# A Perceiver layer on one core: the attention product in one PSUM bank, three banks for projections, another order of steps

## The reference

```python
x = x + cross_attention(layernorm(x), ctx, ctx, mask)   # 16 heads of 16 features, 1601 keys
x = x + span_attention(layernorm(x))                    # 64 positions, scores from a learned distance
x = x + ffn(layernorm(x))                               # shared gated MLP and two hashed experts

# cross attention, all matmuls in float32 accuracy
qh, kh, vh = heads(q @ wq.T + bq), heads(ctx @ wk.T + bk), heads(ctx @ wv.T + bv)
scores = einsum('bhqd,bhkd->bhqk', qh, kh) / 4          # masked with -1e9
out = einsum('bhqk,bhkd->bhqd', softmax(scores), vh)
return merge_heads(out) @ wo.T + bo
```

## Time and profile before

| | us |
|---|---|
| median of 3 runs | 1679.22 |
| lowest and highest run | 1673.58, 1679.73 |
| the profiled execution | 1684.18 |
| its span, first to last instruction | 1682.3 |
| TensorE busy | 1557.7 (93%) |
| VectorE busy | 1049.9 (62%) |
| ScalarE busy | 924.1 (55%) |
| GpSimd busy | 425.0 (25%) |

### The profile page before, as it was taken

The page is one execution under the profiler, slowest core; times in us unless marked ns, Lnnn a source line. Parts: engine busy times, 40 slices in busy tenths (PEclk is TensorE's granted clock), DMA queues, the critical chain, the costliest instruction groups (busy, mean ns, idle before and its releaser), DMA issues. The chain is left out here.

```text
span 1682.3 us, 56731 instructions
## 1 busy us (share of the span) xinstructions
PE 1557.7 (93%) x23644; PEld 1275.9 (76%) x23644; DVE 1049.9 (62%) x3925; ACT 924.1 (55%) x1832; POOL 425.0 (25%) x549
## 2 busy tenths in 40 slices
PE   7699999999999999999999999999999757886997
PEld 2578888888888888888888888888888613333997
DVE  5666666666666666666666666666666446552543
ACT  4355555565555555555565556555555514554553
POOL 0132332222222333323233222222232030000520
PEclk9899999999999999999999999999999978887999
DMA  5433344444444443334334444444443050000111
GB/s 145 138 102 103 104 106 122 124 111 113 110 112 117 110 117 105 105 104 105 104 104 104 120 126 111 112 112 113 112 111 80 9 149 1 1 1 1 51 33 51
DMA packets 101904, 157.94 MB, mean 94 GB/s; under 512 B 56943, under 2 KB 65903, under 8 KB 101376
## 3 DMA queue, kind: packets, MB, share of 16 engines
q1 hardware_dynamic: 101456, 153.69, 34.4%
q0 software_dynamic: 192, 0.59, 0.1%
HBM read 69.17 MB, written 4.19 MB: 44 GB/s over the span
## 5 line engine op out<-in xcount | busy, mean ns | idle before, releaser
L674 DVE CUSTOM_DVE_ANT_0 junk<-bank,mask_q 128x400 bf16<-128x400 f32 (+1 forms) x1024 | 559.0, 571 | 138.9 <-issue 132.3
L626 ACT ACTIVATE probs<-bank 128x512 f32<-128x512 f32 (+1 forms) x832 | 451.1, 595 | 237.9 <-PE bank L786 212.1
L602 POOL CAST ctx_hi<-ctx_raw 128x400 fp32r<-128x400 f32 x248 | 121.6, 519 | 898.2 <-PE bank L750 898.2
L665 DVE SCALAR_TENSOR_TENSOR k_lo<-bank,bk,k_hi 128x400 f16<-128x400 f32 (+1 forms) x256 | 162.4, 634 | 247.3 <-ACT k_hi L636 247.3
L767 PE MATMUL bank<-kstack,qstack 96*128 96x400 f16 (+1 forms) x1024 | 296.8, 339 | 11.4 <-DVE part_max L674 3.8
L750 PE MATMUL bank<-wv_hi,ctx_hi 128*128 128x256 f32 (+1 forms) x832 | 284.3, 342 | 14.4 <-DVE k_lo L665 14.4
L786 PE MATMUL bank<-qstack,kstack 104*128 104x128 f16 (+1 forms) x3328 | 257.9, 220 | 4.1 <-ACT probs L626 3.4
L605 POOL TENSOR_TENSOR ctx_lo<-ctx_raw,ctx_hi 128x400 fp32r<-128x400 f32 x248 | 253.3, 1042 | 0.0
L786 PEld LDWEIGHTS bank<-qstack,kstack 104*128 104x128 f16 (+1 forms) x3328 | 209.1, 99 | 51.0 <-issue 21.6
L646 ACT ACTIVATE v<-bank 128x256 f32<-128x256 f32 (+1 forms) x416 | 159.7, 384 | 148.4 <-PE bank L750 148.3
L636 ACT ACTIVATE k_hi<-bank,bk 128x400 f16<-128x400 f32 (+1 forms) x256 | 152.4, 595 | 158.6 <-PE bank L740 154.2
(11 more groups left out here) (165 smaller groups left out, 1767.0 us busy)
## 6 DMA issues: line engine op xcount, KB each, us to landing
ctx_raw<-in_ctxT SPq DMA_DIRECT2D x32, 1602.0 KB, 7.0
kstack<-k_hi SPq DMA_DIRECT2D x512, 100.1 KB, 2.2
kstack<-k_lo SPq DMA_DIRECT2D x256, 100.1 KB, 2.2
weight<-in_w SPq DMA_DIRECT2D x18, 256.0 KB, 2.7
x<-in_xT SPq DMA_DIRECT2D x8, 512.0 KB, 6.1
attn_out<-o_norm SPq DMA_DIRECT2D x256, 8.0 KB, 1.8
qstack<-q_parts SPq DMA_DIRECT2D x192, 16.0 KB
out_yT<-x SPq DMA_DIRECT2D x1, 2048.0 KB, 6.4
```

What stands on the lines that cost most here:

```text
L602: nc.gpsimd.tensor_copy(c_hi[:, k, s0:s0 + n], raw[:, k, s0:s0 + n]).then_inc(ctx_hi, 1)
L626: nc.scalar.activation(probs[kt % NP][0:m, GROUPS * h:GROUPS * (h + 1), :], st[h][0:m, :], ACT.Exp, scale=DK ** -0.5 / (UP * UP)).then_inc ...
L665: nc.vector.scalar_tensor_tensor(k_lo[:, t, s0:s0 + n], pj[(b.slot + c) % 2][:, 0:n], w["bk"][:, t:t + 1], k_hi[:, t, s0:s0 + n], ALU.add, ...
L674: nc.vector.tensor_tensor_reduce(junk[(b.slot + i) % 2][:, 0:n], sm[(b.slot + i) % 2][:, 0:n], w["mask_q"][:, s0:s0 + n], 1.0, -3.0e38, AL ...
```

## The change

- `ob` is one bank in place of two. A new step O has VectorE copy the finished product of the batch before out of it, to `o_raw` in SBUF (`copy_out`); the first product of a batch waits for that copy (`o_copied`).
- The bank that this frees goes to `pj`: three banks, `bank[0]`, `bank[1]` and `bank[4]`. `sm` becomes `bank[5:7]`. A projection now waits for the one three before it.
- `outputs` works in SBUF on half the columns. The two heads of a pair are joined with two columns of zeros and ones (`half_rows`, a new constant), then the sums are shuffled and inverted, and the last product writes `attn_out` directly. `store` and its 8 DMAs a turn are gone, and the output projection in `tail` waits for `out_done`.
- `SLOTS` is new, so all engines have another order.

```diff
-    pj = bank[0:2]
+    pj = bank[0:2] + bank[4:5]
     st = bank[2:4]
-    sm = bank[4:6]
-    ob = bank[6:8]
+    sm = bank[5:7]
+    ob = bank[7]
...
-    SLOTS = ["K S0 S1 L K", "K S0 S1 K", "K S0 S1 K P P", "K S0 S1 K V",
-             "M V M S0 S1 M V M M P P", "M M S0 S1 M V M", "H M V M S0 S1 M V M M P P", "M M S0 S1 M V M",
-             "H M V M S0 S1 M V M M P P", "M M S0 S1 M V M", "H M V M S0 S1 M V M M P P", "S0 S1 G T V N",
-             "H S0 S1 P P"]
+    SLOTS = ["K K K S0 L S1", "K S0 S1", "K K S0 S1 O K K", "S0 M P P P M M S1", "V S0 M S1 M P M V", "M M V M S0 H M S1 V",
+             "M S0 M V M M P P S1 M M", "V M S0 V M S1 V M V M H", "M S0 S1 M V M", "M S0 V M M S1 V", "S0 M P P M M H V M S1",
+             "V S0 M M S1 P P P G H", "P T S0 N S1"]
...
-            if cur and cur.n >= 2:
-                store(at(cur.n - 2))
...
+        def copy_out(b):
+
+            dve.wait_ge(pv_done, KT * (b.n + 1))
+            nc.vector.tensor_copy(o_raw[:], ob[:, 0:GROUPS * S].rearrange("p (k e c) -> p k e c", k=NK, e=2)).then_inc(o_copied, 1)
+
         def outputs(b):
-            o = ob[b.slot][:, 0:GROUPS * S].rearrange("p (t c) -> p t c", t=GROUPS)
-            dve.wait_ge(pv_done, KT * (b.n + 1))
-            for e in range(2):
-                nc.vector.stream_shuffle(sums[:, e::2, :], o[:, e::2, :], [DK * (1 - e) + i % DK for i in range(32)]).then_inc(sums_done, 1)
-            dve.wait_ge(sums_done, 2 * (b.n + 1))
-            nc.vector.reciprocal(rsum[:], sums[:]).then_inc(rsum_done, 1)
+
+
+            o = [o_raw[:, :, e, :] for e in range(2)]
+            low, high = w["half_rows"][:, 0:1], w["half_rows"][:, 1:2]
+            dve.wait_ge(o_copied, b.n + 1)
+            nc.vector.tensor_scalar(o_half[:], o[1], high, None, ALU.mult).then_inc(halves_done, 1)
+            nc.vector.tensor_scalar(sum_half[:], o[0], high, None, ALU.mult).then_inc(halves_done, 1)
+            dve.wait_ge(halves_done, 2 * (b.n + 1))
+            nc.vector.scalar_tensor_tensor(o_both[:], o[0], low, o_half[:], ALU.mult, ALU.add).then_inc(both_done, 1)
+            nc.vector.scalar_tensor_tensor(sum_both[:], o[1], low, sum_half[:], ALU.mult, ALU.add).then_inc(both_done, 1)
+            dve.wait_ge(both_done, 2 * (b.n + 1))
+            nc.vector.stream_shuffle(sum_half[:], sum_both[:], [(i + DK) % 32 for i in range(32)]).then_inc(sums_done, 1)
+            dve.wait_ge(sums_done, b.n + 1)
+            nc.vector.reciprocal(rsum[:], sum_half[:]).then_inc(rsum_done, 1)
             dve.wait_ge(rsum_done, b.n + 1)
-
-            need(dve, attn_st[b.slot], 16 * STORE_DMAS * (b.used - 1))
-            nc.vector.tensor_tensor(o_norm[b.slot][:], o, rsum[:], ALU.mult).then_inc(out_done, 1)
+            nc.vector.tensor_tensor(attn_out[:, :, b.n * S:(b.n + 1) * S], o_both[:], rsum[:], ALU.mult).then_inc(out_done, 1)
...
-            if j < 2:
-                need(pe, v_done, KT * (b.n - 1) + KT - 1 + j)
-            elif j - 2 < NCK:
-                pe.wait_ge(klo_done, NCK * b.n + j - 1)
+            if j < PJ:
+                need(pe, v_done, KT * (b.n - 1) + KT - PJ + 1 + j)
+            elif j - PJ < NCK:
+                pe.wait_ge(klo_done, NCK * b.n + j - PJ + 1)
             else:
-                pe.wait_ge(v_done, KT * b.n + j - 1 - NCK)
+                pe.wait_ge(v_done, KT * b.n + j - PJ + 1 - NCK)
...
             if kt == 0:
 
-                need(pe, out_done, b.n - 1)
+                need(pe, o_copied, b.n)
...
         def output_a(c, _):
-            for stored in attn_st:
-                pe.wait_ge(stored, 16 * STORE_DMAS * (CB // 2) * (c + 1))
+            pe.wait_ge(out_done, CB * (c + 1))
```

More of the change, by code:

```diff
@@ L47 @@
 VB = 3 * DK
-STORE_DMAS = 2 * GROUPS
 EPS = 1e-5
@@ L120, in build @@
         bo_all = ctx.enter_context(nc.sbuf_tensor("bo_all", [P, NK], F32))
-        attn_st = [sem(f"attn_st{i}") for i in range(2)]
+        out_done = sem("out_done")
         eps_col = ctx.enter_context(nc.sbuf_tensor("eps_col", [P, 1], F32))
@@ L263, in sync @@
             load(bo[:], ins["bo"], wo_in)
+            load(w["half_rows"][:], ins["c_half_rows"], wo_in)
             for c in range(NCH):
@@ L566, in lay_out_keys @@
                                  part[32 * g:32 * g + 32, t, :]).then_inc(kstack_in[b.slot][p], 16)
-        def store(b):
-            sp.wait_ge(out_done, b.n + 1)
-            for g in range(GROUPS):
-                for e in range(2):
-                    rows = slice(32 * g + DK * e, 32 * g + DK * (e + 1))
-                    sp.dma_start(attn_out[rows, :, bass.ds(b.n * S, S)], o_norm[b.slot][rows, e::2, :]).then_inc(attn_st[b.slot], 16)
         sp.wait_ge(first_in["stack_zero"], 2)
@@ L590, in sync @@
         turns(sp, turn)
-        for n in (B - 2, B - 1):
-            store(at(n))
     def gpsimd(pool):
@@ L712, in turn @@
                         shift_in(nxt)
+                    if what == "O" and cur and not first(cur):
+                        copy_out(before(cur))
                     if what == "N" and cur and not first(cur):
@@ L772, in turn_shift @@
             pe.wait_ge(max_found, b.n + 1)
-            nc.tensor.matmul(sm[b.slot][0:PAIRS, 0:P], row_max[:], w["turn_down"][:], start=True, stop=True).then_inc(shift_rows, 1)
+            nc.tensor.matmul(sm[SHIFT_BANK][0:PAIRS, 0:P], row_max[:], w["turn_down"][:], start=True, stop=True).then_inc(shift_rows, 1)
         def scores(b, kt, h, masked):
@@ L800, in products @@
                     c0 = VB * p + DK * e
-                    mm = nc.tensor.matmul(ob[b.slot][32 * g:32 * g + 32, t * S:(t + 1) * S],
+                    mm = nc.tensor.matmul(ob[32 * g:32 * g + 32, t * S:(t + 1) * S],
                                           v[b.slot][0:m, kt, c0:c0 + 2 * DK], probs[kt % NP][0:m, p, S * e:S * (e + 1)],
@@ L936, in _, with span_attention @@
                 mlps["tensor"](pe)
[L939 removed]
+def span_attention(nc, own, bank, sem, mean_w, eps_col, attn_out, out_done, x, h2, wo, bo_all, wspan, wval, wout,
                    sel_a, sel_b, head_ones, x_in, w_in, sel_in, h2_done):
@@ L1511, in constants @@
     return {
+        "c_half_rows": (rows[:, None] % 32 // DK == np.arange(2)[None]).astype(np.float32),
         "c_ident": np.eye(P, dtype=np.float32),
```

54 lines of the change are left out of this document (31 added, 23 removed).

## The result

| | before | after |
|---|---|---|
| median | 1678.88 us | 1627.93 us |
| lowest and highest of 4 runs | 1673.58, 1679.73 | 1625.23, 1629.14 |
| ratio, 95% interval | | 0.9701, 0.9677 to 0.9725 |
| profiled execution, its span | 1684.18, 1682.3 | 1627.13, 1624.9 |

The change saves 51 us, where 42.9 were forecast (1637 us, range 1618 to 1660). I take the span apart by the same marks as in the prediction: the first and the last T, TensorE's last matmul of the last turn, the first matmul of the next part.

A forecast was written before the change was run, and what follows sets the result against it. TensorE, busy 93% of the span, sets the end, with short stalls and passages to win. Terms: 31 x (0.72 + 0.40 + 0) = 34.7, + 5.7 + 2.0 + 0.5 = 42.9 us saved; forecast 1637 us, range 1618 to 1660.

The forecast's parts named there:

- Third bank: Projection V1 waits for K7's low part with two projection banks; a third bank removes that stall, 0.72 us a turn.
- M's waits: M steps wait for VectorE's maximum, 0.75 us a turn; spreading them over the slots leaves 0.35, a gain of 0.40.
- Passages: Cost on TensorE of passing between kinds of step; the new order's changes sum to 0 a turn, bounds -0.3 and +0.5 us.
- One P run -0.1: Entry in the passage sum: the new order has one run of P steps less, saving 0.1 us a turn.
- N and K3: Normalizing on VectorE takes 2.6 us, with the copy 3.0, hidden while K3 finds K0's low part done; cover 0.4 us.
- rival (a): Waits come back elsewhere, before K3 and M0, with dearer V after S: gain 0.6 us a turn, 1652 us; chance 0.15.
- Slices and M0: M0 moves up to 12.0 us behind T; its key slice lands at 11.4, so cover is 0.6 us.
- Stores: Eight store DMAs a turn leave SP's queue: nothing gained within a turn, 5.7 us less in the gap to the next part.
- Last turn: From last T to TensorE's end, set by ScalarE's exponentials: 24.4 becomes 22.4 us, -2.0, bounds -3 and 0.
- First turn: Three projection banks save two short waits for `k_lo` in the first turn, -0.5 us.
- Rival (b): M0 waits for its key slice behind context and query loads: at 2.5 us late, slower at 1695 us; chance 0.05.
- Rival (c): New order doesn't remove stalls, M steps stay gated by VectorE; only V1's 0.72 us and the end remain, 1649 us; chance 0.09.

The follow-up runs named there:

- split_run: The changed kernel with step P8 moved ahead of V12, so the run of four P before T becomes three, with one more P run; 1632.27 us.
- few2_last: The changed kernel with a second order of few passages, P runs mostly two or three long, and the last turn's own order; 1598.82 us, ratio to before 0.9516.
- the longer N: The changed kernel with the reciprocal of the normalizing done twice, some 0.98 us more on VectorE ahead of K0's low part; 1651.07 us.

## Why the prediction came out as it did, by its own steps

The time was inside the range, and the mechanisms were the right ones but for the sum of the passages. The gain was 8 us larger than forecast, and the terms missed by more than that: +16 us in the median turn, -5 for stalls and the shorter first period, -2 for the last turn.

- *Third bank.* Right: 0.72 us a turn forecast, and V1's three steps lost 0.73 in the medians. Between before and the kernel with the old order it is 0.81, which holds the rest of the change as well.
- *M's waits.* Right: gain 0.40 forecast, about 0.45 measured. The laid-out rest of 0.35 us a turn is 0.3 in the rows.
- *Passages.* This is the term that was mis-sized: "0, bounds -0.3 and +0.5" was -0.37 us a turn, 11 us in all, and so outside its own bounds. V behind S was right: 1056.05 - 1055.06 = 0.99 us for S and V, where S takes 0.235 and V 0.71, so 0.045 (0.04 taken). Three other entries of the list failed. "One P run -0.1" is -0.25, as split_run prices one more run. The list left out that the run which ends at T costs nothing to leave: three P take 1.48 us in front of M and 1.36 in front of T (few2_last), so -0.12. And it left out K in front of P, which is 0.1 more than K in front of K (1.27 to 1.29 against 1.18, both behind S) and which the trace of before has once in every turn. These make -0.15 - 0.12 - 0.10 = -0.37, an estimate. K behind S (0.08, and 0.04 taken, from a row where K behind K took 1.13; its median is 1.10) and K behind P (0.10, and 0.08 taken) were too low both, and cancel. By what the prediction worked out from the Trainium skill (TensorE: Matmul & The Clock Gate, Step-by-step) the seven places S to V are free; the rows show 0.045 us for each, so it is not borne out.
- *N and K3.* Size off, not decisive: N took 2.78 and the copy 0.42, 3.2 in place of 3.0. "Cover 0.4 us" was 0.19 by the starts and about 0.1 by the longer N. A little more on VectorE would have been lost time, as rival (a) said; K3 did not wait.
- *Slices and M0.* Right: T + 12.1 (12.0), first issue T + 7.9 (8.0), cover 0.7 (0.6), shown by the queue that was delayed by 5.7 us. Once in 31 turns a slow issue on SyncE used it up, and M0 lost 0.7 us.
- *Stores.* Right: -6.0 in place of -5.7 at the end and nothing in a turn, at their old place. The 0.85 us to the next matmul was 0.33, and VectorE's 3.0 us behind TensorE were 3.3.
- *Last turn.* Wrong in size and in sign: -2.0 forecast, +0.2 measured; the same order takes 23.5 to 24.9 us in three executions, the old one 23.1 and 24.4, so the order made no difference that these few executions show. The step that failed here is that a run of three P keeps ScalarE waiting "0.7 to 1.2 us". It was 2.0 at the first of them, where TensorE had waited itself and ran at a lower clock: the three P take 2.41 us here and 1.55 in an ordinary turn, and the granted clock of the stretch is 0.88. The last turn of before had a lower clock too (0.79 in 1322 to 1330 us), so it is the layout at full clock that was wrong here, not a loss that is new.

```profile
1276.12 2.41 PE L809 MATMUL bank<-probs,v 128*32 128x64 f32 x96
...
1278.90 1.69 ACT L620 ACTIVATE probs<-bank 128x512 f32<-128x512 f32 x3 [2.01 <-PE bank L794]
...
1053.23 1.55 PE L809 MATMUL bank<-probs,v 128*32 128x64 f32 x96
...
1276.00:1284.00 8.00, 6.60 (x226) 5.48 (x224) 1.42 (x3) 4.67 (x10) 0.00 (x0) 0.88 0.02 4
```

- *First turn.* The -0.5 came out, but by luck: from one kernel to the next the first T moves by up to 4 us.
- *Not in the sum.* Irregular stalls, some 4.2 us over 31 turns. They hide part of the gain of the passages: it is 31 x 1.63 = 50.5 by medians and 45.7 in fact. What the stalls don't explain of the difference is that the first period was 2.3 us shorter than the others before and only 0.9 after.

Rival (a) named the right places, but the waits did not come back (0.6 us a turn was its gain, 1.47 the measured one). Rival (b) is a true mechanism whose condition was not met: the slice was there in time. Rival (c) falls: M's waits are down to 0.3 us a turn at the same busy time of VectorE.

## What to carry to other kernels

Where one engine sets the end and has almost no idle time, list every pair of neighbouring steps with its start-to-start time, both for the step in front and for the one behind, before and after the change. It was worth 0.37 us a turn here, beside 0.45 for M's waits. The list of waits shows it at most as short idle times filed under issue (P's were 17.1 us in 600 to 1200 us before and 9.6 after), which are easily passed over. An order is worth something only with the rest of the change that it was laid out for: alone it cost 3%. For things in a queue that nobody waits for, the place decides: eight stores behind the key slices cost nothing in a turn, and ahead of them 6.2 us. So ask of each queue what stands ahead of the first thing that is needed. Where a wait grows past what the trace before had, look at the granted clock behind it as well; it cost 1.6 us a turn on top of a wait of 4.8.
